# Step order and score banks of a fused attention kernel: all four score pairs first, three PSUM banks for each kind

## What is computed

```
q, k, v = split(h @ w_in.T)                       # h: modulated layer norm of x
scores  = q @ k.T * 16 ** -0.5, masked above the diagonal
x       = x + ga * (softmax(scores) @ v @ w_out.T + b_out)
h       = layernorm(x) * (1 + cb) + sb
xr, xk  = mu * h + (1 - mu) * h_prev
x       = x + gb * sigmoid(xr @ W_r.T) * (relu(xk @ W_k.T) ** 2 @ W_v.T)
```

## Time and profile before

| | |
|---|---|
| median of 3 runs | 1637.72 us |
| lowest, highest | 1636.66, 1642.67 us |
| the profiled execution | 1644.7 us |
| its span | 1642.3 us |
| mean granted TensorE clock | 0.911 |
| TensorE busy | 1439.9 us, 88% |
| VectorE busy | 1046.9 us, 64% |
| ScalarE busy | 997.0 us, 61% |
| GpSimd busy | 661.3 us, 40% |

### The profile page before, as it was taken

The page is one execution under the profiler, slowest core; times in us unless marked ns, Lnnn a source line. Parts: engine busy times, 40 slices in busy tenths (PEclk is TensorE's granted clock), DMA queues, the critical chain, the costliest instruction groups (busy, mean ns, idle before and its releaser), DMA issues.

```text
span 1642.3 us, 30240 instructions
## 1 busy us (share of the span) xinstructions
PE 1439.9 (88%) x10856; PEld 816.5 (50%) x10856; DVE 1046.9 (64%) x2082; ACT 997.0 (61%) x1987; POOL 661.3 (40%) x888
## 2 busy tenths in 40 slices
PE   3688899989998899989998899989998899999865
PEld 2454445545554555545555455545555455544344
DVE  3566665766666766666677666676677666766233
ACT  3046555676666666676566766676666766666533
POOL 3102221353435534353445534354444524443454
PEclk7588789999999999989899999989999999999668
DMA  3221123211231223212232222311232222221000
GB/s 109 40 69 47 47 53 93 67 44 47 67 107 49 60 63 93 77 32 57 55 110 59 50 60 70 91 52 49 60 112 62 50 51 72 64 60 48 34 27 26
DMA packets 79508, 101.91 MB, mean 62 GB/s; under 512 B 22512, under 2 KB 43256, under 8 KB 79360
## 3 DMA queue, kind: packets, MB, share of 16 engines
q1 hardware_dynamic: 76544, 91.86, 21.5%
q0 software_dynamic: 2240, 7.34, 1.2%
q10 hardware_dynamic: 576, 0.79, 0.3%
HBM read 30.69 MB, written 8.94 MB: 24 GB/s over the span
## 4 chain that ended last, share of the span: by engine, by line
PE 56%; POOL 12%; DVE 9%; ACT 8%; issue 7%; SPq 5%; DMA 3%; ACTq 0%; POOLq 0%; DVEq 0%
PE col_ps L1116 14%; PE val_ps L1185 12%; PE row_ps L1153 8%; PE dense_ps L1195 7%; SPq L476 5%; PE dense_ps L1196 5%; PE dense_ps L1197 5%; ACT weights L753 4%; DVE max_a L935 3%; POOL weights L626 3%; PE row_ps L1164 2%; DMA xq<-in_x 2%; POOL mix_out L703 1%; POOL xq L706 1%; PE dense_ps L1214 1%
## 5 line engine op out<-in xcount | busy, mean ns | idle before, releaser
L753 ACT ACTIVATE weights<-col_ps 128x512 f32<-128x512 f32 (+2 forms) x1280 | 641.8, 554 | 342.2 <-PE col_ps L1116 327.9
L935 DVE TENSOR_REDUCE max_a<-row_ps 128x1 f32<-128x512 f32 (+3 forms) x896 | 535.6, 644 | 238.2 <-PE row_ps L1164 122.9
L1116 PE MATMUL col_ps<-q_stack,k_stack 64*128 64x512 f32 (+3 forms) x1536 | 426.5, 435 | 42.9 <-ACT weights L753 40.6
L1153 PE MATMUL row_ps<-k_stack,q_stack 62*128 62x512 f32 (+3 forms) x1536 | 372.9, 428 | 28.2 <-DVE max_a L935 20.5
L626 POOL TENSOR_SCALAR_AFFINE_SELECT weights<-weights 128x512 f32<-128x512 f32 x256 | 164.2, 641 | 552.8 <-ACT weights L753 551.5
L1185 PE MATMUL val_ps<-weights,v_ones 128*32 128x512 f32 (+3 forms) x3072 | 354.2, 535 | 34.8 <-POOL weights L626 34.0
L1116 PEld LDWEIGHTS col_ps<-q_stack,k_stack 64*128 64x128 f32 x1536 | 203.7, 197 | 312.7 <-ACT weights L753 292.1
L935 DVE TENSOR_REDUCE max_b<-row_ps 128x1 f32<-128x384 f32 (+3 forms) x384 | 214.4, 594 | 187.8 <-PE row_ps L1164 187.8
L1153 PEld LDWEIGHTS row_ps<-k_stack,q_stack 62*128 62x128 f32 x1536 | 182.3, 198 | 143.2 <-DVE max_a L935 66.7
L1164 PE MATMUL row_ps<-mask_fill,mask_ident 64*128 64x128 bf16 (+1 forms) x2048 | 146.0, 214 | 0.0
L1185 PEld LDWEIGHTS val_ps<-weights,v_ones 128*32 128x32 f32 x3072 | 62.3, 111 | 127.6 <-POOL weights L626 59.8
(11 more groups left out here) (164 smaller groups left out, 2122.5 us busy)
## 6 DMA issues: line engine op xcount, KB each, us to landing
q_stack<-q_part SPq DMA_DIRECT2D x384, 64.0 KB, 2.2
k_stack<-k_part SPq DMA_DIRECT2D x372, 64.0 KB, 2.2
xa<-in_x SPq DMA_DIRECT2D x8, 1024.0 KB, 5.8
att<-val_out SPq DMA_DIRECT2D x64, 128.0 KB
recips<-recip_rows SPq DMA_DIRECT2D x32, 256.0 KB
xq<-in_x SPq DMA_DIRECT2D x28, 256.0 KB, 3.2
out<-xq POOLq DMA_DIRECT2D x28, 256.0 KB, 2.7
q_stack<-max_rows SPq DMA_DIRECT2D x256, 4.0 KB
```

The costliest lines, as they stand in the source:

```text
L753: nc.scalar.activation(weights[:, t % 2, heads[0]:heads[-1] + 1:2, 0:q1 - q0], col_ps[bank][:, 0:n * (q1 - q0)].rearrange("p (h q) -> p h ...
L935: nc.vector.reduce_max(dest, bank[:, 0:len(heads) * (k1 - k0)].rearrange("p (h k) -> p h k", h=len(heads)), AX_X).then_inc(max_done, 1)
L1116: last = nc.tensor.matmul(col_ps[bank][:, i * (q1 - q0):(i + 1) * (q1 - q0)], stack_at(k_stack[s % 2], rows, heads[i], P * j, P * (j + 1)) ...
L1153: last = nc.tensor.matmul(banks[odd][:, n * width:(n + 1) * width], stack_at(q_stack[stack], rows, heads[n], P * i, P * (i + 1)), stack_at ...
```

## The change

Column scores get three banks and row scores three. On TensorE the second row pair (with mt0) and the second column pair come straight after the first column pair, and the values of the step before come after them, ahead of the dense units. On VectorE both early row units are reduced first, and all late ones ahead of the mixing. In the drain the dense units of the last quarter use the third column bank, and its first one waits for all exponentials.

```diff
-COL_BANKS, ROW_BANKS = 2, 4
+COL_BANKS, ROW_BANKS = 3, 3
...
         def dense_of(bb, s):
 
-            return row_ps[s][:].rearrange("p (a n) -> p a n", a=2) if bb == B else dense_ps[:]
+            bank = (row_ps + col_ps[2:])[s]
+            return bank[:].rearrange("p (a n) -> p a n", a=2) if bb == B else dense_ps[:]
...
-                    for u in early[:1]:
+                    for u in early:
                         maximum(b, s, u)
                     rest_of_qk(b, kind, s, t)
                     for item in at:
                         empty_dense(*item)
-                    for u in early[1:]:
+                    for u in late:
                         maximum(b, s, u)
                     for item in at:
                         mix(*item, 0)
-                    for u in late:
-                        maximum(b, s, u)
                     for item in at:
                         mix(*item, 1)
                         back(*item)
...
-                    if name == "out":
+                    if name == "out" and s == G - 1:
+                        pe.wait_ge(exp_done, exp_index(B, 0, 0))
+                    elif name == "out":
                         pe.wait_ge(max_done, unit_index(B - 1, G - 2, MT1) + 1)
...
                     row_scores(b, s, early)
                     for c in cols[:1]:
                         score_columns(b, s, t, c)
+                    row_scores(b, s, late)
+                    for c in cols[1:]:
+                        score_columns(b, s, t, c)
                     if attends(kind) if t else has_late(kind, s):
                         values(*last)
-                    for c in cols[1:]:
-                        score_columns(b, s, t, c)
-                    row_scores(b, s, late)
```

## The result

The changed kernel takes 1701.02 us (median of 4 runs, 1687.24 to 1708.81) beside 1640.2 us of the kernel before; the ratio is 1.034, 95% interval 1.027 to 1.042. That is the forecast side and inside the whole range (1618 to 1712), but 61 us where 27 were forecast, and above the forecast's own range (1648 to 1688). The profiled execution took 1701.15 us, with a span of 1698.7 us and a mean granted clock of 0.897 (before 0.911).

The account below looks back on a forecast made before the run. TensorE's in-order sequence and its short bank waits bound the kernel. Step changes of +2.1 us a section net to +0.8, +25 over 31 sections, plus 2 for the last: +27 on 1637.7 gives 1665 us, range 1618 to 1712.

Parts of the forecast that it names:

- R2's second half waits for the first reduction of its step: Second row pair's second half takes the step's first row bank: issues 1.45 us into step 6, 1.37 into step 2.
- steps 2, 3 and 9: Wide first reduction with little beside it, so the second row pair waits: +0.52, +0.5 and +0.5 us.
- Step 4: Narrow first reduction, 128-wide value product that covers little: dense unit at 2.41 us instead of 2.85, -0.44 us.
- C2's second half waits for the first exponential, and V covers nothing: Second column pair's second half goes 1.41 us into step 5; the value product, now behind it, covers no wait.
- steps 5 and 8: No second row pair; second column pair waits for the first exponential: +0.39 us in step 5, step 8 likewise.
- Steps 0 and 4: Steps predicted to get shorter: -0.4 us in step 0, -0.44 us in step 4.
- Steps 6 and 7: 512-wide value product now behind the second column pair: step 6 from 2.83 to 3.08 us, +0.25; step 7 likewise.
- Credits: Per section: -1.2 us for values waiting for GpSimd, -0.3 for first row pair behind VectorE, +0.2 for late reductions and exponentials.
- Rival C: Much slower: the row bank ties TensorE to VectorE's lateness within a step, +3.0 us a section, 1733 us; chance 0.18.
- Rival A: Faster: local losses vanish in waits the next step has anyway, about -34 us, 1606 us; chance 0.24.
- step 10: Only first row pair, first column pair and values, order unchanged: 0 before credits.
- What would show it: Weight-load waits: columns well below 292 us, values below 15, rows above 200; dense unit in step 4 near 2.4 us.

Follow-up runs that it names:

- short reductions: Each row-score reduction reads only the first quarter of its columns, in the changed kernel (1592.91 us) and in the kernel before (1594.2 us).
- the filler: Changed kernel with the first matmul of each second row pair issued two times more ahead of itself, result overwritten: 1663.42 us, ratio 1.013.
- banks alone: Kernel before with three column and three row banks and the drain edit, old order on TensorE and VectorE: 1651.13 us, ratio 1.003.
- values second in 5 and 8: Changed kernel with values again behind the first column pair where a step has no late row pair: 1686.96 us, ratio 1.024.

## Why the prediction was right, and where it was too small

- *R2's second half waits for the first reduction of its step.* Right to 0.02 us in steps 2 and 6. With short reductions steps 2, 3 and 9 get most of it back, and the whole distance goes. Step 4 has a second wait of this kind, of mt0 for the second reduction, that the forecast left out: D at 2.60 instead of 2.41.
- *C2's second half waits for the first exponential, and V covers nothing.* Right to 0.04 us in step 5. At full clock steps 5 and 8 cost 0.6 us each on average instead of 0.39. In the second section of a batch, where ScalarE does other work first, they cost 1.80 and 1.57, with the clock falling in both. This is the local term that was sized too small: one quiet step stood for all.
- *Steps 0 and 4 gain.* -0.34 and -0.44 in length, forecast -0.40 and -0.44. For step 4 that is partly luck: D comes only 0.25 us earlier in the first section of a batch.
- *Steps 6 and 7 lose 0.25 each.* Wrong in the mean: -0.24 and +0.08. In the quiet step 6 the loss is there (3.13 to 2.83); in other sections the kernel before was the late one: in step 6 of the fourth section C2 waited there for ScalarE, and D goes 3.12 us in where it went at 4.45.
- *Credits: 1.2 us for V's wait, 0.3 for R1's, 0.2 against.* The values' wait fell by 30.7 us by the matmuls, 1.0 us a section, and by 55.4 by the weight loads, 1.7; 1.2 was taken. Net 1.2 us at full clock to a forecast of 0.8. That the sums agree so well is partly luck: the forecast is off by 0.2 to 0.5 us, in both directions, in steps 2, 5, 6, 8, 9 and 10, and the misses partly cancel.
- *The clock* is the term that was missing: forecast 0, by the aligned steps 16 to 27 of the 52 us in the middle six batches; the filler, which undoes more than the added half-clock time, gives 38. The forecast spoke of idle time only as time. I had the granted clock at hand, and read no row of it.
- Rival C priced a late VectorE. The time came out between the forecast and it, but for another reason: step 9, its place, lost 0.2 us at full clock, and banks alone cost nothing. The engine that was late was ScalarE, in steps 5 and 8. Rival A's mechanism (the next step takes the loss back) is seen in step 10, -0.53 (in the first and third sections of a batch step 9 takes 0.76 us more and step 10 1.0 less), and in step 6 of the run with the values second in 5 and 8.
- *What would show it.* Column waits 100.4 us, well below 292; values 4.4 us at the weight loads behind GpSimd, below 15; row waits 201.5 us, above 200; step 4 at 2.60, where "near 2.4" was asked for. The first was a weak sign: the column matmuls themselves idle 56.8 us, more than the 40.6 before.

## What to carry to other kernels

Between the issue of a matmul and the wait for what another engine makes of it, count what lies over that latency; an order that groups like work together takes the cover away, and a spare bank helps only the side that gets it. Where TensorE waits in every step, price the clock too: compare steps at full clock with all steps, and read the granted clock before trusting a sum of waits. Size a wait over all kinds of section, not in the quietest: here the largest losses stood in steps whose quiet copy lost 0.4 us. A short matmul whose result is thrown away, put into a wait that exists anyway, is a cheap test of it. In the changed kernel it was also a gain of 38 us, in the kernel before none.

## What the runs showed of the hardware

The half-clock share moved with small idle pieces. In the changed kernel TensorE's clock fell 25 times in the middle six batches; 12 of these falls lay in two steps that hold a wait of 1.44 to 1.50 us each, and no wait of scores for VectorE or ScalarE in that kernel was over 1.9 us. Adding two matmuls of up to 0.2 us in eight of twelve steps took the share from 15.4 to 6.9% and 38 us off the time. The Trainium skill, page "TensorE: Matmul & The Clock Gate", section "A second HAM failure mode: psum-queue depth-cycling", says that frequent short idle times between groups of matmuls bring the clock down and cost throughput; the runs of the changed kernel with and without the filler (granted clock 0.97 and 0.92 in the same stretch) agree. The banks alone limit it: there the share rose to 14.6% and the time stayed.
